# A graph attention kernel on one core: where the softmax's row sum is inverted, and which engine adds up the attention output

## The chip, the cores and the metric

The kernel runs on one core of one Trainium2 chip. The metric is the device time of the whole kernel in microseconds; the time before is the median of three runs. All events below are from one profiled execution, in microseconds from the start of its span.

Engines are called by the profile's names: PE (TensorE matmul), PEld (its weight loads), DVE (VectorE), ACT (ScalarE), POOL (GpSimd) and SP (SyncE, which issues DMAs here).

## The reference

There are N = 4096 nodes with D = 128 features, and a 4096x4096 adjacency matrix of int32 (ones and zeros). Two layers are added to x, each on relu(layernorm(x)):

```
h = relu(layernorm(x))                          # layer 1: masked dot-product attention
q, k, v = h @ Wq.T + bq, h @ Wk.T + bk, h @ Wv.T + bv
scores  = where(adj > 0, q @ k.T / sqrt(128), -9e15)
x = x + elu(softmax(scores) @ v)

h = relu(layernorm(x))                          # layer 2: additive attention
hw = h @ W; s1, s2 = hw @ a[:128], hw @ a[128:]
e = where(adj > 0, leaky_relu(s1[:, None] + s2[None, :], 0.01), -9e15)
x = x + hw + softmax(e) @ h
```

The change concerns the end of layer 1 alone: the division by the softmax's row sum, the bias bv (added behind the division, since a softmax row sums to one) and the elu.

## The kernel before

The kernel has four stages, told apart by the time at which they run in the profile.

1. 0 to about 60 us: x comes in, layernorm, and the products that give q, k and v. Each of q, k and v is kept as a high and a low part, so that products of reduced-precision operands keep float32's accuracy.
2. About 60 to 556 us: layer 1. The 4096 rows are T = 32 strips of 128. A strip is one **period** of every engine's program. Periods 0 to 3 and 28 to 31 are written out, and a loop runs over four periods at a time in between (`all_periods`). This is the stage that the change edits.
3. About 556 to 603 us: the second layernorm, the product with W and what depends on it.
4. About 603 to 841 us: layer 2's products (line 1248), strip by strip.

In stage 2 the order of every engine's work is written out by hand in `period(c, b, ahead)`, with s = 4c + b the strip; every engine executes its own list in order, and semaphores join the lists. For one strip:

- **SP** loads adj rows (2 MB of int32) two strips ahead, and stores mask bytes for layer 2.
- **POOL** turns adj into bytes (`make_bytes`, line 493) and bytes into a bf16 mask of 0 or -9e15 (`make_mask`, line 506). A pass takes a whole strip of 4096 columns. It also finishes the elu of the strip two back (`add_elu`, lines 512 to 515) and adds it to x.
- **PE** makes scores in four parts of 1024 columns (`make_scores`, lines 699 to 701, three products for each half), transposes the exponentials in eight blocks of 512 (`transpose(s, b, j)`, line 711), and multiplies each transposed block by v (`times_v(s, j)`, lines 721 and 722), which accumulates in `ps_acc`. Its order is: transpose 0, times_v 6 of the strip before, scores part 2 of s+1, transpose 1, times_v 7 of the strip before, scores part 3 of s+1, transpose 2, times_v 0, transpose 3, times_v 1, scores part 0 of s+2, transpose 4, times_v 2, transpose 5, times_v 3, transpose 6, times_v 4, scores part 1 of s+2, transpose 7, times_v 5.
- **DVE** adds the mask to each scores part and takes its maximum (`add_mask`, line 618, with a small gate at 616), takes the maximum over the parts (`find_max`, 624), and makes the low part of each transposed block (`low_part(s, j)`, line 630). PE's `times_v(s, j)` waits for `low_part(s, j)`. Between `low_part(s, 3)` and the mask addition for s+2 stands `normalise(s - 1)` (lines 633 to 643).
- **ACT** takes the exponentials (line 548, with the row sums), makes the high part of each block (`copy_pT`, 554), copies the accumulator of the strip before to SBUF behind block 1 (`acc_copy`, 560), and behind block 7 computes relu and exp for the elu (`elu_exp`, 565 to 568).

The accumulator has two halves of 128 columns, from the high and low parts of v. `normalise` takes the sum of four partial row sums (line 636), its reciprocal (637), adds the halves in SBUF (641), and multiplies by the reciprocal and adds the bias (642). The result `att` goes to ACT's `elu_exp`. A `Steps` helper puts a wait on DVE's own semaphore behind an instruction whose result the next one reads. `ps_acc` is one buffer: PE's `times_v(s, 0)` waits until ACT has copied strip s-1's accumulator.

Of the kernel before, what the change touches and what calls it, by code (L numbers as in the profile page):

```python
# [18 lines left out]
D = 128  # L19
# [217 lines left out]
def build(nc, x, adj, wq, bq, wk, bk, wv, bv, w1, a1, out):  # L237
# [7 lines left out]
    with ExitStack() as whole:  # L245
# [21 lines left out]
        row_sum = sb(whole, "row_sum", [D, 4, NP], F32)  # L267
        pool_gate = sb(whole, "pool_gate", [D, 5], F32)
        table_gate = sb(whole, "table_gate", [D, 3], F32)
        gate = sb(whole, "gate", [D, 4 * NP + 1], F32)  # L270
        inv_sum = sb(whole, "inv_sum", [D, 2], F32)

        const_ready, loaded, x_in = sem("const_ready"), sem("weights_loaded"), [sem(f"x_in{c}") for c in range(NC)]
# [10 lines left out]
        with ExitStack() as first:  # L284
# [7 lines left out]
            with ExitStack() as c1:  # L292
# [126 lines left out]
                sem("acc_out"), sem("att_ready"), sem("att_exp_ready"), sem("epilogue_done"))  # L419
            att_cut = sem("att_cut")  # L420
            own, pool_own = sem("vector_steps"), sem("pool_steps")
            gate_ready = sem("pool_gate_ready")
            bytes_ready, m_stored = sem("mask_bytes_ready"), [sem("even_masks_stored"), sem("odd_masks_stored")]
            STEPS = 3

            with ExitStack() as c2:
# [53 lines left out]
                def _(pool):  # L480
# [14 lines left out]
                    def make_mask(c, b):  # L495
# [10 lines left out]
                        nc.gpsimd.tensor_scalar(out, src, -NEG, NEG, ALU.mult, ALU.add).then_inc(mask_ready, 1)  # L506

                    def add_elu(s):

                        steps = Steps(pool, pool_own, 2 * s)  # L510
                        pool.wait_ge(att_exp_ready, s + 1)
                        steps.do(nc.gpsimd.tensor_tensor(att_exp[:], att_exp[:], ones[:], ALU.subtract))  # L512
                        steps.do(nc.gpsimd.tensor_tensor(att_exp[:], att_exp[:], att_pos[:], ALU.add))
                        xs = x_sb[:, s, :] if isinstance(s, int) else x_sb[:, bass.ds(s, 1), :].rearrange("p o f -> p (o f)")
                        nc.gpsimd.tensor_tensor(xs, xs, att_exp[:], ALU.add).then_inc(epi_done, 1)
# [7 lines left out]
                    def period(c, b, ahead):  # L523
                        last = isinstance(c, int) and c == NC - 1
                        if not (isinstance(c, int) and 4 * c + b < 2):
                            add_elu(4 * c + b - 2)
                        if not (last and b > 1):
                            make_mask(c + (b + 2) // 4, (b + 2) % 4)
                        if not (last and b > 0):
                            make_bytes(c + (b + 3) // 4, (b + 3) % 4)  # L530

                    all_periods(pool, period)
                    add_elu(T - 2)
                    add_elu(T - 1)

                @block.scalar
                def _(act):
# [17 lines left out]

                    def acc_copy(s):

                        act.wait_ge(pv_done, 8 * s + 8)
                        wait(act, att_ready, s)
                        nc.scalar.activation(acc_sb[:], ps_a[:], ACT.Copy).then_inc(acc_out, 1)  # L560

# [13 lines left out]
                    def period(c, b, ahead):  # L575
# [7 lines left out]
                        if not first:  # L583
                            acc_copy(s - 1)
                        copy_pT(s, 2)
# [15 lines left out]
                    all_periods(act, period)  # L601
                    acc_copy(T - 1)
                    elu_exp(T - 1)
# [3 lines left out]
                def _(dve):  # L607
# [24 lines left out]

                    def normalise(s, b):

                        steps = Steps(dve, own, STEPS * s)
                        steps.do(nc.vector.tensor_reduce(out=inv_sum[:, 0:1], in_=row_sum[:, b, :], axis=AX.X, op=ALU.add))
                        steps.do(nc.vector.reciprocal(inv_sum[:, 1:2], inv_sum[:, 0:1]))
                        dve.wait_ge(acc_out, s + 1)
                        wait(dve, att_exp_ready, s)
                        wait(dve, epi_done, s)  # L640
                        steps.do(nc.vector.tensor_tensor(acc_sb[:, 0, :], acc_sb[:, 0, :], acc_sb[:, 1, :], ALU.add))
                        nc.vector.scalar_tensor_tensor(out=att[:], in0=acc_sb[:, 0, :], scalar=inv_sum[:, 1:2], in1=bv_rep[:],
                                                       op0=ALU.mult, op1=ALU.add).then_inc(att_ready, 1)

# [13 lines left out]
                    def period(c, b, ahead):  # L658
                        s, bn = 4 * c + b, (b + 1) % 4
                        first = isinstance(c, int) and c == 0 and b == 0  # L660
                        low_part(s, 0)
                        if ahead:
# [6 lines left out]
                        low_part(s, 3)  # L669
                        if not first:  # L670
                            normalise(s - 1, (b + 3) % 4)
                        if ahead == 2:
# [6 lines left out]
                        low_part(s, 7)  # L679
                        if not first and not (isinstance(c, int) and s < 2):  # L680
                            moments_of(s - 2)

                    all_periods(dve, period)
                    normalise(T - 1, 3)
                    moments_of(T - 2)
                    dve.wait_ge(epi_done, T)
                    moments_of(T - 1)

# [615 lines left out]
```

## Time and profile before

| | us |
|---|---|
| median of 3 runs (lowest, highest) | 844.09 (843.63, 844.32) |
| the profiled execution's own time | 843.2 |
| its span, first to last instruction | 841.4 |
| PE busy | 771.5 |
| DVE busy | 618.2 |
| ACT busy | 566.9 |
| POOL busy | 303.6 |
| mean granted TensorE clock | 0.981 of full speed |

Matmuls are pipelined and their ends are modelled: the next one can start before the modelled end of the one in front, so the start-to-start distance tells what a matmul costs, and an idle time shown before a matmul begins at the modelled end. Idle times in square brackets are those of the engine, with what ended them.

### The profile page before, as it was taken

To read this page: it belongs to the slowest core of one execution; us is meant where nothing else is said; L and a number is where in the kernel's file an instruction comes from. 1 tells how busy PE (TensorE), PEld (TensorE's weight loads), DVE (VectorE), ACT (ScalarE), POOL (GpSimd) and SP (SyncE) were. 2 spreads that over 40 slices of the span, in tenths; PEclk is the share of its full clock that TensorE was granted. 3 is DMA by queue.
4 is the path that set the end of the run, shared out by engine and by line. 5 is a ranking of instruction groups with operands and counts; after the bars stand their busy time and mean duration, and the time that the engine had idled before them with its cause. 6 is when DMAs were issued, how large, how long until landed. Compare 5 with 4: busy or idle time off the path is not lost. (4 is left out here: it accounts for less than half of the span.)

```text
span 841.4 us, 17904 instructions
## 1 busy us (share of the span) xinstructions
PE 771.5 (92%) x6229; PEld 657.5 (78%) x6229; DVE 618.2 (73%) x1358; ACT 566.9 (67%) x1159; POOL 303.6 (36%) x238
## 2 busy tenths in 40 slices
PE   4979999999999999999999999968599999999997
PEld 2558888788788788788888888856488888888886
DVE  4847778778778778778778778659856755775672
ACT  5937767667667667667657657758588779777911
POOL 1087466466466466465465463124200000000000
PEclk9979999999999999999999999979799999999999
DMA  8069353643643543544544510045023344333200
GB/s 306 8 205 361 135 176 127 213 163 125 212 162 129 207 162 132 205 162 135 207 157 137 208 54 26 1 86 116 1 58 85 74 83 99 68 73 87 60 10 11
DMA packets 83338, 105.67 MB, mean 126 GB/s; under 512 B 68448, under 2 KB 75104, under 8 KB 79200
## 3 DMA queue, kind: packets, MB, share of 16 engines
q1 hardware_dynamic: 82560, 104.87, 39.8%
q8 instruction: 24, 0.39, 0.2%
q10 hardware_dynamic: 576, 0.26, 0.1%
q14 instruction: 18, 0.15, 0.1%
q0 software_dynamic: 160, 0.00, 0.0%
HBM read 69.47 MB, written 18.87 MB: 105 GB/s over the span
## 5 line engine op out<-in xcount | busy, mean ns | idle before, releaser
L554 ACT ACTIVATE pT_high<-ps_t 128x512 bf16<-128x512 f32 x256 | 151.8, 594 | 158.5 <-PE ps_t L711 157.6
L1248 PE MATMUL ps_x<-v,big 128*128 128x258 bf16 x2048 | 231.9, 274 | 2.3 <-issue 2.3
L1248 PEld LDWEIGHTS ps_x<-v,big 128*128 128x128 fp8e4 x2048 | 198.9, 98 | 32.5 <-issue 2.4
L721 PE MATMUL ps_acc<-v_parts,pT_high 128*128 128x256 bf16 x1024 | 196.7, 273 | 27.7 <-DVE pT_low L630 27.4
L618 DVE CUSTOM_DVE_ANT_0 scores<-ps_s,mask_neg 128x1024 f32<-128x1024 f32 x128 | 156.2, 1221 | 71.7 <-issue 71.7
L630 DVE TENSOR_TENSOR pT_low<-ps_t,pT_high 128x512 bf16<-128x512 f32 x256 | 171.3, 687 | 20.3 <-ACT pT_high L554 17.1
L722 PE MATMUL ps_acc<-v_parts,pT_low 128*128 128x128 bf16 x1024 | 182.7, 219 | 0.0
L548 ACT ACTIVATE scores<-scores,neg_max 128x1024 f32<-128x1024 f32 x128 | 146.2, 1144 | 13.6 <-DVE neg_max L624 13.6
L711 PE MATMUL ps_t<-ident,scores 128*128 128x128 f32 x1024 | 154.3, 273 | 0.5 <-DVE pT_low L630 0.5
L789 ACT ACTIVATE big<-s_block,s_col 128x512 fp8e4<-128x512 f32 x224 | 139.7, 718 | 0.0
L721 PEld LDWEIGHTS ps_acc<-v_parts,pT_high 128*128 128x128 bf16 x1024 | 100.1, 98 | 44.1 <-DVE pT_low L630 35.0
L711 PEld LDWEIGHTS ps_t<-ident,scores 128*128 128x128 f32 x1024 | 117.0, 140 | 18.7 <-DVE pT_low L630 0.5
L699 PE MATMUL ps_s<-k_hi,q_strip 128*128 128x512 f32 x256 | 113.0, 441 | 5.0 <-DVE row_max L618 2.8
L506 POOL TENSOR_SCALAR mask_neg<-mask_bytes 128x4096 bf16<-128x4096 uint8 x32 | 115.4, 3605 | 2.3
L493 POOL TENSOR_SCALAR mask_bytes<-adj_sb 128x4096 uint8<-128x4096 int32 x32 | 115.2, 3599 | 1.2 <-DMA mask_bytes_dram<-mask_bytes 0.6
L701 PE MATMUL ps_s<-k_hi,q_strip 128*128 128x512 f32 x256 | 102.3, 400 | 0.0
L722 PEld LDWEIGHTS ps_acc<-v_parts,pT_low 128*128 128x128 bf16 x1024 | 100.2, 98 | 2.5
L700 PE MATMUL ps_s<-k_lo,q_strip 128*128 128x512 f32 x256 | 101.3, 396 | 0.0
L512 POOL TENSOR_TENSOR att_exp<-att_exp,ones 128x128 f32<-128x128 f32 x32 | 14.6, 457 | 216.1 <-ACT att_exp L568 216.1
L1183 ACT ACTIVATE sums<-ps_x,ac 128x258 f32<-128x258 f32 x64 | 26.7, 469 | 63.8 <-PE ps_x L1248 63.8
L699 PEld LDWEIGHTS ps_s<-k_hi,q_strip 128*128 128x128 f32 x256 | 49.2, 192 | 12.9 <-DVE row_max L618 3.5
L701 PEld LDWEIGHTS ps_s<-k_hi,q_strip 128*128 128x128 f32 x256 | 49.0, 191 | 11.7
(133 smaller groups left out, 733.1 us busy)
## 6 DMA issues: line engine op xcount, KB each, us to landing
adj_sb<-in_adj SPq DMA_DIRECT2D x32, 2048.0 KB, 8.0
mask_bytes_dram<-mask_bytes SPq DMA_DIRECT2D x32, 512.0 KB, 8.7
x_sb<-in_x SPq DMA_DIRECT2D x8, 256.0 KB, 8.1
out<-res SPq DMA_DIRECT2D x32, 64.0 KB, 1.5
big<-mask_bytes_dram SPq DMA_TRANSPOSE x32, 4.5
raw_w<-in_L_gnn_Wq ACTq DMA_DIRECT2D x1, 64.0 KB, 3.1
raw_w<-in_L_gnn_Wk ACTq DMA_DIRECT2D x1, 64.0 KB, 3.6
raw_w<-in_L_gnn_Wv ACTq DMA_DIRECT2D x1, 64.0 KB, 4.9
```

The lines of the kernel that those rows point to most:

```text
L506: nc.gpsimd.tensor_scalar(out, src, -NEG, NEG, ALU.mult, ALU.add).then_inc(mask_ready, 1)
L548: nc.scalar.activation(sc, sc, ACT.Exp, bias=neg_max[:, bn:bn + 1], accum_out=row_sum[:, bn, k:k + 1]).then_inc(exp_done, 1)
L554: nc.scalar.activation(pT_high[j % 4][:], ps_t[j % 3][:], ACT.Copy).then_inc(pT_ready, 1)
L618: nc.vector.tensor_tensor_reduce(out=scores[bn % 2][:, part], in0=ps_s[k % 2][:], in1=mask[bn % 2][:, part], scale=1.0, scalar=LOWEST, op0 ...
L630: nc.vector.tensor_tensor(pT_low[j % 4][:], ps_t[j % 3][:], pT_high[j % 4][:], ALU.subtract).then_inc(low_ready, 1)
L699: nc.tensor.matmul(o, q[:, 0, :], k_hi[:, col], start=True, stop=False)
L701: last = nc.tensor.matmul(o, q[:, 1, :], k_hi[:, col], start=False, stop=True)
L711: last = nc.tensor.transpose(ps_t[j % 3][:, D * i:D * i + D], scores[b % 2][:, col:col + D], ident[:])
L721: nc.tensor.matmul(ps_a[:], pT_high[j % 4][:, part], v_parts[:, t, :, :], start=(t == 0), stop=False)
L722: last = nc.tensor.matmul(ps_a[:, 0, :], pT_low[j % 4][:, part], v_parts[:, t, 0, :], start=False, stop=(t == T - 1))
L789: return nc.scalar.activation(by_key_tile(lower[par], t), src.rearrange("p (s i) -> p s i", s=4), ACT.Sign, bias=s_col[:, t, 1:2], saturat ...
L1248: last = nc.tensor.matmul(ps_x[b % 2][k][:], by_key_tile(m, t)[:, b], v1[k][:, t, :].bitcast(BF16), start=(t == 0), stop=(t == T - 1))
```

## The change

`normalise` is taken apart. The sum of the row sums and its reciprocal (now `inverse_sum`) stand at the start of a period on DVE, and the reciprocal goes into a buffer with one column for odd and one for even strips. ACT's copy of the accumulator multiplies by it (`scale=`), so both halves arrive divided. POOL adds the halves and then the bias (`add_halves`), between its mask pass and its bytes pass. DVE's bn_stats for the second layernorm (`moments_of`) runs three strips behind instead of two, with a wait on the elu's end.

```diff
-        pool_gate = sb(whole, "pool_gate", [D, 5], F32)
+        pool_gate = sb(whole, "pool_gate", [D, 9], F32)
+        inv_by_parity = sb(whole, "inv_by_parity", [D, 2], F32)
...
-            STEPS = 3
+            STEPS = 1
...
+                    def add_halves(s, b):
+
+                        pool.wait_ge(acc_out, s + 1)
+                        if not isinstance(s, int):
+                            nc.gpsimd.tensor_tensor(pool_gate[:, 5 + b:6 + b], pool_gate[:, 0:1], pool_gate[:, 0:1], ALU.add)
+                        wait(pool, att_exp_ready, s)
+                        nc.gpsimd.tensor_tensor(acc_sb[:, 0, :], acc_sb[:, 0, :], acc_sb[:, 1, :], ALU.add).then_inc(halves_added, 1)
+                        pool.wait_ge(halves_added, s + 1)
+                        nc.gpsimd.tensor_tensor(att[:], acc_sb[:, 0, :], bv_rep[:], ALU.add).then_inc(att_ready, 1)
...
                             make_mask(c + (b + 2) // 4, (b + 2) % 4)
+                        if not (isinstance(c, int) and 4 * c + b < 1):
+                            add_halves(4 * c + b - 1, (b - 1) % 4)
                         if not (last and b > 0):
                             make_bytes(c + (b + 3) // 4, (b + 3) % 4)
 
                     all_periods(pool, period)
                     add_elu(T - 2)
+                    add_halves(T - 1, 3)
                     add_elu(T - 1)
...
-                    def acc_copy(s):
+                    def acc_copy(s, b):
 
                         act.wait_ge(pv_done, 8 * s + 8)
                         wait(act, att_ready, s)
-                        nc.scalar.activation(acc_sb[:], ps_a[:], ACT.Copy).then_inc(acc_out, 1)
+                        act.wait_ge(inv_ready, s + 1)
+                        nc.scalar.activation(acc_sb[:], ps_a[:], ACT.Copy, scale=inv_by_parity[:, b % 2:b % 2 + 1]).then_inc(acc_out, 1)
...
-                    def normalise(s, b):
+                    def inverse_sum(s, b):
 
                         steps = Steps(dve, own, STEPS * s)
                         steps.do(nc.vector.tensor_reduce(out=inv_sum[:, 0:1], in_=row_sum[:, b, :], axis=AX.X, op=ALU.add))
-                        steps.do(nc.vector.reciprocal(inv_sum[:, 1:2], inv_sum[:, 0:1]))
-                        dve.wait_ge(acc_out, s + 1)
-                        wait(dve, att_exp_ready, s)
-                        wait(dve, epi_done, s)
-                        steps.do(nc.vector.tensor_tensor(acc_sb[:, 0, :], acc_sb[:, 0, :], acc_sb[:, 1, :], ALU.add))
-                        nc.vector.scalar_tensor_tensor(out=att[:], in0=acc_sb[:, 0, :], scalar=inv_sum[:, 1:2], in1=bv_rep[:],
-                                                       op0=ALU.mult, op1=ALU.add).then_inc(att_ready, 1)
+                        wait(dve, acc_out, s - 1)
+                        nc.vector.reciprocal(inv_by_parity[:, b % 2:b % 2 + 1], inv_sum[:, 0:1]).then_inc(inv_ready, 1)
...
                         first = isinstance(c, int) and c == 0 and b == 0
+                        if not first:
+                            inverse_sum(s - 1, (b + 3) % 4)
                         low_part(s, 0)
...
                         low_part(s, 2)
                         low_part(s, 3)
-                        if not first:
-                            normalise(s - 1, (b + 3) % 4)
...
                         low_part(s, 7)
-                        if not first and not (isinstance(c, int) and s < 2):
-                            moments_of(s - 2)
+                        if not (isinstance(c, int) and s < 3):
+                            dve.wait_ge(epi_done, s - 2)
+                            moments_of(s - 3)
 
                     all_periods(dve, period)
-                    normalise(T - 1, 3)
-                    moments_of(T - 2)
-                    dve.wait_ge(epi_done, T)
-                    moments_of(T - 1)
+                    inverse_sum(T - 1, 3)
+                    for s in range(T - 3, T):
+                        dve.wait_ge(epi_done, s + 1)
+                        moments_of(s)
```

On DVE, in the middle of period 3 (the last one written out before the loop), before the change: the two `low_part` for blocks 2 and 3, `normalise`, the mask addition for part 0 of strip 5 (lines 616 and 618), and the `low_part` for blocks 4 to 6.

```order
L630 TENSOR_TENSOR pT_low<-ps_t,pT_high 128x512 [waits pT_ready] x2
L636 TENSOR_REDUCE inv_sum<-row_sum 128x1
L637 RECIPROCAL inv_sum<-inv_sum 128x1 [waits vector_steps]
L641 TENSOR_TENSOR acc_sb<-acc_sb 128x128 [waits att_exp_ready,epilogue_done,acc_out,vector_steps]
L642 SCALAR_TENSOR_TENSOR att<-acc_sb,inv_sum,bv_rep 128x128 [waits vector_steps]
L616 MEMSET gate 128x1 [waits scores_ready,p_transposed,mask_ready]
L618 ISA scores,row_max<-ps_s,mask_neg 128x1024
L618 ISA row_max 128x1
L630 TENSOR_TENSOR pT_low<-ps_t,pT_high 128x512 [waits pT_ready] x3
```

The same place with the change; `low_part` is now at line 645 and the mask addition at 631 and 633.

```order
L645 TENSOR_TENSOR pT_low<-ps_t,pT_high 128x512 [waits pT_ready] x2
L631 MEMSET gate 128x1 [waits scores_ready,p_transposed,mask_ready]
L633 ISA scores,row_max<-ps_s,mask_neg 128x1024
L633 ISA row_max 128x1
L645 TENSOR_TENSOR pT_low<-ps_t,pT_high 128x512 [waits pT_ready] x3
```

All four instructions have left this place. Two of them stand at the start of the period, between `low_part(s - 1, 7)` and `low_part(s, 0)`:

```order
L645 TENSOR_TENSOR pT_low<-ps_t,pT_high 128x512 [waits pT_ready]
L651 TENSOR_REDUCE inv_sum<-row_sum 128x1
L653 RECIPROCAL inv_by_parity<-inv_sum 128x1 [waits acc_out,vector_steps]
L645 TENSOR_TENSOR pT_low<-ps_t,pT_high 128x512 [waits pT_ready]
L631 MEMSET gate 128x1 [waits scores_ready,p_transposed]
L633 ISA scores,row_max<-ps_s,mask_neg 128x1024
```

DVE no longer waits for `acc_out` of the strip just copied, only for that of the strip before it.

On POOL, one period before the change: three steps of the elu, the mask pass and the bytes pass.

```order
L512 TENSOR_TENSOR att_exp<-att_exp,ones 128x128 [waits att_exp_ready]
L513 TENSOR_TENSOR att_exp<-att_exp,att_pos 128x128 [waits pool_steps]
L515 TENSOR_TENSOR x_sb<-x_sb,att_exp 128x128 [waits pool_steps]
L506 TENSOR_SCALAR mask_neg<-mask_bytes 128x4096 [waits scores_masked,mask_bytes_ready]
L493 TENSOR_SCALAR mask_bytes<-adj_sb 128x4096 [waits odd_masks_stored,adj_in_odd]
```

And with it:

```order
L523 TENSOR_TENSOR att_exp<-att_exp,ones 128x128 [waits att_exp_ready]
L524 TENSOR_TENSOR att_exp<-att_exp,att_pos 128x128 [waits pool_steps]
L526 TENSOR_TENSOR x_sb<-x_sb,att_exp 128x128 [waits pool_steps]
L507 TENSOR_SCALAR mask_neg<-mask_bytes 128x4096 [waits scores_masked,mask_bytes_ready]
L515 TENSOR_TENSOR acc_sb<-acc_sb 128x128 [waits att_exp_ready,acc_out]
L517 TENSOR_TENSOR att<-acc_sb,bv_rep 128x128 [waits acc_halves_added]
L494 TENSOR_SCALAR mask_bytes<-adj_sb 128x4096 [waits odd_masks_stored,adj_in_odd]
```

Two additions have come in, the first of which waits for ACT's copy; in the loop a gate of one column (`pool_gate`) stands before them. The bytes pass is queued behind them. ACT's and PE's lists keep their order.

## Rows read from the trace of the kernel before

**Rows 1.** Windows: busy us of each engine, granted clock, DMA share, GB/s.
```profile
61.00:552.00 491.00, 462.83 (x3802) 403.53 (x3802) 389.71 (x814) 330.34 (x694) 264.14 (x199) 1.00 0.45 155
612.00:841.00 229.00, 223.42 (x2018) 194.58 (x2015) 143.31 (x310) 160.00 (x290) 0.00 (x0) 1.00 0.30 65
```

**Rows 2.** Waits of PE, stage 2's largest: us in total, times, longest.
```profile
PE ps_acc L721 <- DVE pT_low L630: 27.4, 30, 1.0
```

**Rows 3.** Timeline of PE: start us, us, what; first, a middle, last stall.
```profile
102.08 0.28 PE L721 MATMUL ps_acc<-v_parts,pT_high 128*128 128x256 bf16 x1 [0.55 <-DVE pT_low L630]
...
304.49 0.61 PE L711 MATMUL ps_t<-ident,scores 128*128 128x128 f32 x4
306.10 0.28 PE L721 MATMUL ps_acc<-v_parts,pT_high 128*128 128x256 bf16 x1 [1.00 <-DVE pT_low L630]
...
510.17 0.28 PE L721 MATMUL ps_acc<-v_parts,pT_high 128*128 128x256 bf16 x1 [0.55 <-DVE pT_low L630]
```

**Rows 4.** Timeline of DVE ahead of the stall at 306.10.
```profile
300.23 1.49 DVE L630 TENSOR_TENSOR pT_low<-ps_t,pT_high 128x512 bf16<-128x512 f32 x2
301.64 0.15 DVE L636 TENSOR_REDUCE inv_sum<-row_sum 128x1 f32<-128x4 f32 x1
...
302.08 1.75 DVE L641 TENSOR_TENSOR acc_sb<-acc_sb 128x128 f32<-128x128 f32 x1
...
304.20 1.23 DVE L618 CUSTOM_DVE_ANT_0 scores<-ps_s,mask_neg 128x1024 f32<-128x1024 f32 x1
...
305.36 1.88 DVE L630 TENSOR_TENSOR pT_low<-ps_t,pT_high 128x512 bf16<-128x512 f32 x3
```

**Rows 5.** Timeline of POOL, bytes pass, elu and mask pass.
```profile
300.09 3.60 POOL L493 TENSOR_SCALAR mask_bytes<-adj_sb 128x4096 uint8<-128x4096 int32 x1
310.12 0.46 POOL L512 TENSOR_TENSOR att_exp<-att_exp,ones 128x128 f32<-128x128 f32 x1 [6.43 <-ACT att_exp L568]
...
311.99 3.61 POOL L506 TENSOR_SCALAR mask_neg<-mask_bytes 128x4096 bf16<-128x4096 uint8 x1
```

**Rows 6.** Timeline of DVE, line 641 in periods 1, 2, 29 and 30.
```profile
83.91 0.29 DVE L641 TENSOR_TENSOR acc_sb<-acc_sb 128x128 f32<-128x128 f32 x1
...
98.45 1.43 DVE L641 TENSOR_TENSOR acc_sb<-acc_sb 128x128 f32<-128x128 f32 x1
...
521.83 0.29 DVE L641 TENSOR_TENSOR acc_sb<-acc_sb 128x128 f32<-128x128 f32 x1
...
536.38 0.29 DVE L641 TENSOR_TENSOR acc_sb<-acc_sb 128x128 f32<-128x128 f32 x1
```

**Rows 7.** Timeline: copy of block 4, accumulator copy, PE's times_v 0.
```profile
303.17 0.58 ACT L554 ACTIVATE pT_high<-ps_t 128x512 bf16<-128x512 f32 x1
...
313.15 0.39 ACT L560 ACTIVATE acc_sb<-ps_acc 128x256 f32<-128x256 f32 x1
...
314.82 0.27 PE L721 MATMUL ps_acc<-v_parts,pT_high 128*128 128x256 bf16 x1
```

**Rows 8.** Timeline of DVE where a period starts.
```profile
310.82 0.69 DVE L630 TENSOR_TENSOR pT_low<-ps_t,pT_high 128x512 bf16<-128x512 f32 x1 [0.38 <-ACT pT_high L554]
312.06 1.22 DVE L618 CUSTOM_DVE_ANT_0 scores<-ps_s,mask_neg 128x1024 f32<-128x1024 f32 x1 [0.55 <-issue]
```

**Rows 9.** Single lines: duration ns min/median/max, first and last start.
```profile
L630 DVE TENSOR_TENSOR pT_low<-ps_t,pT_high x256: 678/686/694, 64.8 to 550.8; 128x512 bf16<-128x512 f32 x128
L1183 ACT ACTIVATE sums<-ps_x,ac x64: 454/470/481, 613.1 to 835.8; 128x258 f32<-128x258 f32 x64
```

**Rows 10.** Timeline of the end of stage 2: POOL, DVE, ACT.
```profile
552.01 0.45 POOL L513 TENSOR_TENSOR att_exp<-att_exp,att_pos 128x128 f32<-128x128 f32 x1
552.54 0.45 POOL L515 TENSOR_TENSOR x_sb<-x_sb,att_exp 128x128 f32<-128x128 f32 x1
553.13 0.29 DVE L641 TENSOR_TENSOR acc_sb<-acc_sb 128x128 f32<-128x128 f32 x1 [1.15 <-POOL x_sb L515]
...
553.84 0.31 ACT L565 ACTIVATE att_neg<-att 128x128 f32<-128x128 f32 x1 [1.00 <-DVE att L642]
```

More of the change, by code:

```diff
@@ L419, in build @@
                 sem("acc_out"), sem("att_ready"), sem("att_exp_ready"), sem("epilogue_done"))
-            att_cut = sem("att_cut")
-            own, pool_own = sem("vector_steps"), sem("pool_steps")
+            att_cut, halves_added = sem("att_cut"), sem("acc_halves_added")
+            own, pool_own, inv_ready = sem("vector_steps"), sem("pool_steps"), sem("inv_sum_ready")
             gate_ready = sem("pool_gate_ready")
             bytes_ready, m_stored = sem("mask_bytes_ready"), [sem("even_masks_stored"), sem("odd_masks_stored")]
-            STEPS = 3
+            STEPS = 1
             with ExitStack() as c2:
@@ L583, in period @@
                         if not first:
-                            acc_copy(s - 1)
+                            acc_copy(s - 1, b + 1)
                         copy_pT(s, 2)
@@ L601, in _ @@
                     all_periods(act, period)
-                    acc_copy(T - 1)
+                    acc_copy(T - 1, 3)
                     elu_exp(T - 1)
```

## The prediction, made blind

> **What bounds the kernel now.** I read the windows by stage first. Stage 2, from 61 to 552 us, is 491 us long; PE is busy for 463 of them at a granted clock of 1.00, DVE for 390, ACT for 330, POOL for 264 [rows 1]. So PE bounds the stage, and what can be had without less matmul work is about 28 us of pauses. The waits of PE come next: 27.4 us, 30 times, before the first matmul of a `times_v`, on DVE's `low_part` [rows 2]. The timeline of PE says which: once in a period, behind transpose 6, `times_v(s, 4)` begins 1.61 us after it instead of following it at once (304.49 to 306.10, shown as 1.00 us of idle), for want of `low_part(s, 4)` [rows 3].
>
> The timeline of DVE says why that is late [rows 4]. `low_part` 2 and 3 end at 301.72. Then stand the sum and reciprocal (301.64 to 302.08), the addition of the halves at line 641, 1.75 us, line 642, and the mask addition from 304.20; only at 305.36 do `low_part` 4 to 6 run. Block 4 had been copied by ACT at 303.17 + 0.58 = 303.75 [rows 7]. So `low_part(s, 4)` is 1.6 us late.
>
> Line 641 doesn't need 1.75 us. In period 1 it took 0.29 us, in period 29 and 30 too [rows 6]. In the period shown POOL's bytes pass runs from 300.09 to 303.69 [rows 5], and line 641 ends at 302.08 + 1.75 = 303.83, just behind it. The instruction is held until the pass is over. Nothing else on DVE is: the 256 `low_part`, whose one SBUF input is the high part, take 678 to 694 ns throughout, POOL busy or not [rows 9].
>
> The Trainium skill (SBUF — State Buffer, Who interferes with whom) has this as a rule: a DVE instruction with two SBUF inputs and a GpSimd instruction that reads SBUF exclude each other for the whole instruction. The rule would also hold line 642 and spare all that stays on DVE in the loop, where each instruction has at most one SBUF input; the durations agree.
>
> **The size of the stall, from periods without it.** Line 641 starts at 83.91 and 98.45, a period of 14.54 us; at 521.83 and 536.38, 14.55 us [rows 6]. Both have no stall of PE in between. From 98.45 to 521.83 lie 27 periods in 423.38 us, 15.68 each. Each holds one stall, the first at 102.08, the last at 510.17; three show 0.55 us, 24 show 1.00 to 1.03 [rows 3]. Without stalls these 27 periods would take 27 x 14.55 = 392.9 us. The difference is 423.4 - 392.9 = 30.5 us. The sum of the shown idle is a little less, since the modelled end of the transpose hides some 0.17 us of each. The 14.55 us are also a floor: PE has no pause left in such a period, and the change takes nothing off PE.
>
> **The change part by part.**
>
> *Removed from the middle of the period on DVE:* the sum and reciprocal (0.44 us), the held addition (1.75 + 0.04), and line 642 (303.87 to 304.20, 0.33): the whole distance from 301.64 to 304.20, 2.56 us [rows 4]. What is late next? The mask addition for s+2 needs PE's scores part, which ends at about 302.5: it would run from 302.5 to 303.7. Block 4's copy is ready at 303.75, so `low_part(s, 4)` runs 303.75 to 304.44. PE would ask for it 0.44 us after transpose 6 begins, at 304.93. It is there half a microsecond early, and the stall goes completely: -30.5 us. The real periods without a stall say the same, and they had even 0.29 us of line 641 and line 642 in the way.
>
> *Added at the start of the period on DVE:* sum and reciprocal, 0.44 us by the distance 301.64 to 302.08, and a wait on the copy of the strip before the last, nearly a period old. Queued behind it is `low_part(s, 0)`, which now waits 0.38 us for ACT and has another 0.55 us of idle behind it before the mask addition, which waits for PE's scores [rows 8]. PE needs `low_part(s, 0)` only at `times_v(s, 0)`, 314.82 [rows 7], over 3 us later. Cost 0. If the cover were gone, 0.44 us a period, 31 x 0.44 = 14 us, is the upper bound.
>
> *ACT's copy with a scale:* 0.39 us without [rows 7]. With a scale from a column, ACT's copies of the same kind in layer 2 take 0.47 us for 258 columns [rows 9], so +0.08. It would end at 313.62; PE's `times_v(s, 0)` wants it at 314.82 [rows 7]. Hidden, with 1.2 us to spare. The new wait on the reciprocal is met 2 us before, and the one on `att_ready` now asks for POOL's addition of the period before: due about 11 us earlier. Cost 0 in the loop.
>
> The Trainium skill (ScalarE: Activation LUTs, What ACT_TABLE_LOAD costs) has a scale or bias read from a column at about 93 ns more than an immediate; by that the copy would take an estimated 0.48 us, which changes nothing in the sum.
>
> *POOL's two additions:* the elu's additions of the same shape take 0.46 us and follow each other at 0.53 to 0.54 us [rows 5, 10]. With a gate of a column (0.26 us) the two take 1.3 us, behind the mask pass, which ends at 315.60 [rows 5]. ACT's copy is there at 313.6, so POOL needn't wait. `att` is ready at about 316.9; ACT's elu wants it seven microseconds later, at the period's end. POOL's work in a period becomes about 1.9 (elu and gate) + 3.7 + 1.3 + 3.9 = 10.8 us, of 14.55. The mask pass stands ahead of the additions and isn't moved; the bytes pass ends 1.3 us later and is read by POOL itself 3.7 us after that, and by the DMAs, which have two periods. Cost 0.
>
> On this edit the Trainium skill speaks against the change: its GPSIMD Engine Reference, 4.1 Engine selection, keeps element-wise additions on VectorE, with GpSimd about two times slower for two inputs. The rows have 0.29 us on DVE undisturbed and 0.46 on POOL; by the rule it would be an estimated 0.58 each, off the critical path as well, but for the tail.
>
> *The moments* go from two strips behind to three: same count, and the wait is on an elu that ended a period before. 0. In the first periods POOL's bytes pass for strip 4 must wait for ACT's copy, some 5 us later than now, with over 8 us until POOL needs it: 0.
>
> *The tail* is on the path: behind the last `times_v` everything waits for everything. Now: POOL's elu for strip 30 ends at 552.99, DVE adds at 553.13, ACT starts at 553.84 [rows 10]. Then: POOL starts its first addition at 553.07, the second 0.53 us later, ends 0.45 us after that at 554.05, ACT at about 554.1. +0.3 us; the bounds are 0 and, with both additions at their unhidden 0.54 + 0.54 and one more handover, +0.5.
>
> **Sum.** -30.5 + 0.3 = -30.2 us. The profiled execution took 843.2 (span 841.4), which gives 813.0 (811.2). The median of the runs shown is 0.9 above it: forecast 813.9 us. Its own range, with bounds of 1.5 us below (the run's own 0.9 and a little idle of DVE and ACT set free in the last, irregular periods) and 3 us above (up to 0.1 us a period of new waits), is 812.4 to 817.
>
> **Rivals.**
>
> *Half of the stall comes back.* The half microsecond that `low_part(s, 4)` has in hand is eaten up, because something else is held on DVE or ACT reaches block 4 later. For it: the margin is small against 1.2 us of stall. Against: periods 1 and 29 had 0.64 us more on DVE at this very place and no stall [rows 6]. If 0.5 us stay in each of 27 periods: 813.9 + 13.5 = 827 us.
>
> *The change doesn't move the stall,* because line 641 was only the place where a late ACT or PE was waited for, and `low_part(s, 4)` takes over the wait. Then it is 844 us, within the 0.2% (1.7 us) that a measurement of this kernel can't tell from none. Against: block 4's copy was ready at 303.75, 1.6 us before it was used [rows 4, 7].
>
> *Slower: a ring through POOL.* ACT's copy waits for POOL's addition of the period before, POOL's addition for ACT's copy, POOL's two passes stand in the same queue, and DVE's mask addition waits for a pass. The place is the gap between POOL's 10.8 us and the period; it decides when POOL's round exceeds 15.7 us, the period of now. For it: POOL's round grows, and its additions read two SBUF tensors while DVE is busy four fifths of the time; if each were held as line 641 was, 1.3 us more each, POOL is at 13.4 us, and a hold of all its five additions, 6.5 us, brings 17.3 us with the mask late. 29 rounds of 17.3 instead of 15.7: 844 + 46 = 890 us at the worst; at 16.2 us a round, 858. Against: POOL's passes take 3.60 and 3.61 us beside a working DVE [rows 5], and its elu additions 0.45 to 0.46 in the loop and at the idle end alike [rows 5, 10].
>
> A fall of the granted clock, now that PE never pauses, would cost too; stage 4 has PE busy 223 of 229 us at 1.00 [rows 1], which speaks against it. I count it with the second rival.
>
> **How the numbers follow.** Forecast 0.87; half of it back 0.07; no change 0.02; slower 0.04. Faster by over 0.2%: 0.87 + 0.07 = 0.94; same 0.02; slower 0.04. For 8 in 10 the range needs the forecast's own with a little more on the side where all the unknowns lie: 812 to 819.
>
> **What would show it.** In the changed profile the wait of PE's `ps_acc` on `pT_low` should be 1 to 3 us in total instead of 27.4, mostly outside the loop; periods should be 14.55 us; no DVE instruction of the loop should vary in length; POOL's additions should take 0.46 us, and POOL should still idle over 3 us before each elu. The accumulator copy should take 0.47 us. The forecast is wrong if `low_part` 4 still ends after 0.44 us behind transpose 6, if PE shows a new wait for ACT's copy, or if PE's clock drops in stage 2.

## The result, and the profile after

| | before | after |
|---|---|---|
| median us (lowest, highest), runs | 844.21 (843.63, 844.52), 4 | 814.33 (811.28, 815.24), 4 |
| ratio (95% interval) | 1 | 0.9641 (0.9615 to 0.9666) |
| profiled execution: own time, span | 843.2, 841.4 | 811.28, 809.5 |

The change makes the kernel 3.6% faster: 29.9 us between the medians. The windows of the changed kernel are cut at its own stage ends. As in [rows 1], a line has the window, its length, the busy us (and instructions) of PE, PEld, DVE, ACT and POOL, the granted clock, the DMA share and GB/s.

```profile
61.00:522.00 461.00, 457.35 (x3798) 404.04 (x3796) 336.49 (x750) 331.87 (x693) 295.15 (x289) 1.00 0.47 164
582.00:809.50 227.50, 221.66 (x2002) 193.06 (x1999) 141.99 (x309) 158.68 (x288) 0.00 (x0) 1.00 0.30 65
```

Stage 2 has PE busy for 457 of 461 us, at the same granted clock. The waits of PE on the accumulator's matmuls, which answer to [rows 2] (us in total, times, longest):

```profile
PE ps_acc L732 <- DVE pT_low L645: 1.6, 3, 0.8
PE ps_acc L732 <- ACT acc_sb L575: 0.2, 1, 0.2
```

27.4 us have become 1.6: three waits of 0.3, 0.5 and 0.85 us in the written-out periods at either end, which the kernel before had too. None is left in the inner periods. The middle of one period on DVE, which answers to [rows 4]; `low_part` is now line 645, the mask addition 633:

```profile
299.16 1.49 DVE L645 TENSOR_TENSOR pT_low<-ps_t,pT_high 128x512 bf16<-128x512 f32 x2
301.44 1.22 DVE L633 CUSTOM_DVE_ANT_0 scores<-ps_s,mask_neg 128x1024 f32<-128x1024 f32 x1 [0.78 <-issue]
301.46 0.06 DVE L631 MEMSET gate<- 128x1 f32 x1
302.58 0.08 DVE L633 DVE_READ_ACCUMULATOR2_ANT row_max<- 128x1 f32 x1
302.70 0.69 DVE L645 TENSOR_TENSOR pT_low<-ps_t,pT_high 128x512 bf16<-128x512 f32 x1
```

DVE has 0.78 us of idle where 2.56 us of work and holding stood (the profile names no releaser for it; PE's last product of this scores part ends at 301.39, just ahead of the mask addition), and `low_part(s, 4)` ends at 303.39. On PE, transpose 6 of the same period and the `times_v(s, 4)` that used to stall, which answer to [rows 3]:

```profile
303.43 0.61 PE L722 MATMUL ps_t<-ident,scores 128*128 128x128 f32 x4
303.87 0.27 PE L732 MATMUL ps_acc<-v_parts,pT_high 128*128 128x256 bf16 x1
```

0.44 us lie between them, not 1.61, and no idle time is shown: `low_part(s, 4)` is 0.48 us ahead of its use. The period's start on DVE, in two successive periods (one row of each for the distance, then what stands behind it), answers to [rows 8]:

```profile
293.57 0.14 DVE L651 TENSOR_REDUCE inv_sum<-row_sum 128x1 f32<-128x4 f32 x1
...
308.12 0.14 DVE L651 TENSOR_REDUCE inv_sum<-row_sum 128x1 f32<-128x4 f32 x1
308.30 0.16 DVE L653 RECIPROCAL inv_by_parity<-inv_sum 128x1 f32<-128x1 f32 x1
308.41 0.69 DVE L645 TENSOR_TENSOR pT_low<-ps_t,pT_high 128x512 bf16<-128x512 f32 x1
309.81 1.22 DVE L633 CUSTOM_DVE_ANT_0 scores<-ps_s,mask_neg 128x1024 f32<-128x1024 f32 x1 [0.70 <-issue]
```

308.12 - 293.57 = 14.55 us, the period. DVE is still idle for 0.70 us, until PE's last product of the scores part ends at 309.77. POOL in the same period, which answers to [rows 5]:

```profile
293.32 0.46 POOL L523 TENSOR_TENSOR att_exp<-att_exp,ones 128x128 f32<-128x128 f32 x1 [4.15 <-ACT att_exp L583]
...
295.19 3.61 POOL L507 TENSOR_SCALAR mask_neg<-mask_bytes 128x4096 bf16<-128x4096 uint8 x1
298.88 0.20 POOL L513 TENSOR_TENSOR pool_gate<-pool_gate 128x1 f32<-128x1 f32 x1
299.02 0.46 POOL L515 TENSOR_TENSOR acc_sb<-acc_sb 128x128 f32<-128x128 f32 x1
299.56 0.46 POOL L517 TENSOR_TENSOR att<-acc_sb,bv_rep 128x128 f32<-128x128 f32 x1
299.98 0.19 POOL L493 TENSOR_TENSOR pool_gate<-pool_gate 128x1 f32<-128x1 f32 x1
300.13 3.60 POOL L494 TENSOR_SCALAR mask_bytes<-adj_sb 128x4096 uint8<-128x4096 int32 x1
```

POOL's round is 10.4 us; in the loop it idles 4.15 us before each elu.

Where the 31.9 us between the two spans lie, by the first `times_v` (before 65.54, after 64.29), the first step of the second layernorm (556.78, 525.35), the first matmul of line 1248, 1259 in the changed kernel (603.48, 572.09), and the end (841.4, 809.5): 1.25 us in stage 1, which the change doesn't touch and where executions of one kernel differ by as much; 491.24 - 461.06 = 30.18 us in stage 2; 46.70 against 46.74 us in stage 3; 0.5 us in stage 4.

### The profile page after: what moved, and what is told of

It reads as the page before. It is cut to its first block and busy times, and to the rows that moved or that the text cites. A ratio compares the mean times of both kernels' runs of the same rounds, so it can differ in the third digit from the quotient of the medians.

```text
span 809.5 us, 17843 instructions
## 1 busy us (share of the span) xinstructions
PE 765.8 (95%) x6229; PEld 658.3 (81%) x6229; DVE 565.6 (70%) x1294; ACT 568.7 (70%) x1159; POOL 335.4 (41%) x326
## 5 line engine op out<-in xcount | busy, mean ns | idle before, releaser
L645 DVE TENSOR_TENSOR pT_low<-ps_t,pT_high 128x512 bf16<-128x512 f32 x256 | 176.3, 690 | 46.7 <-ACT pT_high L568 43.0
```

Source lines behind the costliest of these rows:

```text
L645: nc.vector.tensor_tensor(pT_low[j % 4][:], ps_t[j % 3][:], pT_high[j % 4][:], ALU.subtract).then_inc(low_ready, 1)
```

## The experiments

There were twelve runs, in three sets; each is compared with the kernel before in its own set. A period is a start-to-start distance in the loop. The **block** is what stands on DVE between `low_part(s, 3)` and the mask addition for s+2, from its first instruction's start to the mask addition's, or to its own end where DVE idles behind it.

**The changed kernel again (after_again).** 

> The changed kernel itself, timed again beside the others. All theories: about 814 us, in a span of some 4 us between its runs. It serves as the comparison for the three kernels that run with it.

Measured 815.05 us (814.61 to 815.95, 5 runs) against 843.57: ratio 0.9662 (0.9648 to 0.9676). A third time (after_third), beside the last experiments: 

> The changed kernel, timed once more beside the version with one reduction on DVE. All theories: 814 to 815.5 us.

 It took 813.46 us (811.71 to 816.06, 5 runs), 0.5 below the expected range, ratio 0.9651 (0.9635 to 0.9666).

**One reduction on DVE for halves and bias (e3_three).** An edit of the changed kernel: the bias stands as a third block beside the two halves, which ACT's copy has scaled. (Dots stand for lines that are not shown; the comments say what a line is for.)

```diff
-                acc_sb = sb(c2, "acc_sb", [D, 2, D], F32)
+                acc_sb = sb(c2, "acc_sb", [D, 3, D], F32)      # [:, 2, :] holds the bias
...
+                        nc.vector.tensor_reduce(out=att[:], in_=acc_sb[:].rearrange("p k f -> p f k"), axis=AX.X,
+                                                op=ALU.add).then_inc(att_ready, 1)    # DVE, behind low_part(s, 3)
...
-                            add_halves(4 * c + b - 1, (b - 1) % 4)                    # POOL
```

> The changed kernel, with the halves and the bias added on DVE again, in the old place behind low_part 3, but by one reduction over three blocks of a single SBUF tensor (the two halves and a copy of the bias). Theory (what hurt was that line 641, with two SBUF inputs, was held until POOL's pass ended): the reduction is never held, takes 0.35 to 0.5 us every time, and falls into the 0.78 us in which DVE waits for the scores at this place; PE has no stall, 813.5 to 814.5 us, even 0.3 to 0.5 us below the changed kernel, since the last strip is added without POOL. Rival (any work of DVE between low_part 3 and the mask addition delays low_part 4): 0.4 us a period, 826 us. Rival (POOL's pass holds every DVE instruction that reads the accumulator's copy): 844 us.

Measured 812.92 us, ratio 0.9636 (0.9621 to 0.965), 0.6 below the expected range. The reduction, over 32 calls (duration ns min/median/max, first and last start):

```profile
L647 DVE TENSOR_REDUCE att<-acc_sb x32: 584/589/601, 83.3 to 522.4; 128x128 f32<-128x384 f32 x32
```

It is never held, at the very place where line 641 was held for 1.46 us, and beside POOL's bytes pass as before: in one period it runs from 301.61 to 302.19, the pass from 300.07 to 303.67. (It takes 0.59 us; I had expected 0.35 to 0.5.) PE has no stall in the inner periods: 14.55 us each. So neither a place nor DVE's reading of the accumulator's copy was the matter.

**POOL's bytes pass in eight pieces, all else as before (e1_pieces).**

```diff
-                        nc.gpsimd.tensor_scalar(mask_bytes[b % 2][:], adj_sb[b % 2][:], 1.0, 0.0, ALU.min, ALU.max).then_inc(bytes_ready, 1)
+                        for i in range(8):
+                            piece = slice(512 * i, 512 * i + 512)
+                            last = nc.gpsimd.tensor_scalar(mask_bytes[b % 2][:, piece], adj_sb[b % 2][:, piece], 1.0, 0.0, ALU.min, ALU.max)
+                        last.then_inc(bytes_ready, 1)
```

> The kernel before, with POOL's bytes pass cut into eight passes of 512 columns; DVE keeps all of its work in the old place. Theory: line 641 is held for one piece at the most, so it takes 0.3 to 0.8 us instead of 1.75, PE's stall is gone or below 0.2 us a period, and the time is 814 to 819 us without any of the change. Rival (DVE's work in this place is simply too long, 2.56 us): 835 to 844 us, since only the hold is shorter. Rival (the pieces cost POOL so much that its round becomes the bound): POOL's round of 9.5 us grows by 7 times 0.1 us, no effect.

Measured 817.42 us, ratio 0.9691 (0.9675 to 0.9707). DVE's block in one period and POOL's pieces beside it, and DVE's two instructions over all:

```profile
304.96 0.15 DVE L639 TENSOR_REDUCE inv_sum<-row_sum 128x1 f32<-128x4 f32 x1
...
305.41 0.50 DVE L644 TENSOR_TENSOR acc_sb<-acc_sb 128x128 f32<-128x128 f32 x1
305.94 0.58 DVE L645 SCALAR_TENSOR_TENSOR att<-acc_sb,inv_sum,bv_rep 128x128 f32<-128x128 f32 x1
306.45 1.21 DVE L621 CUSTOM_DVE_ANT_0 scores<-ps_s,mask_neg 128x1024 f32<-128x1024 f32 x1
```
```profile
303.43 4.72 POOL L495 TENSOR_SCALAR mask_bytes<-adj_sb 128x512 uint8<-128x512 int32 x8
```
```profile
L644 DVE TENSOR_TENSOR acc_sb<-acc_sb x32: 291/498/749, 85.5 to 527.1; 128x128 f32<-128x128 f32 x32
L645 DVE SCALAR_TENSOR_TENSOR att<-acc_sb,inv_sum,bv_rep x32: 352/580/585, 85.9 to 527.4; 128x128 f32<-128x128 f32 x32
```

Eight pieces in 4.72 us are 0.59 us each, so one ends at about 305.79 and the next at 306.38; the two instructions end at 305.91 and 306.52. Each of the two instructions with two SBUF inputs is now held for 0.2 us, to the end of a piece, instead of one of them to the end of the pass. The block is 304.96 to 306.45, 1.49 us, the period 14.64. The hold is the cause of most of the stall: 26.2 of the 28.5 us that the change brings in the same set of runs come back with DVE's program untouched. (The pieces cost POOL 1.1 us a period, 4.72 against 3.60, where 0.7 was expected; POOL has the room.)

**The addition as a reduction, line 642 kept (e2_reduce).**

```diff
-                        steps.do(nc.vector.tensor_tensor(acc_sb[:, 0, :], acc_sb[:, 0, :], acc_sb[:, 1, :], ALU.add))
+                        steps.do(nc.vector.tensor_reduce(out=acc_sum[:], in_=acc_sb[:].rearrange("p k f -> p f k"), axis=AX.X, op=ALU.add))
```

> The kernel before, with the addition of the halves as a reduction over one SBUF tensor; line 642 behind it keeps its two SBUF inputs. Theory (two SBUF inputs against a POOL instruction that reads SBUF): the reduction takes 0.3 to 0.4 us, and line 642 is held in its place until POOL's pass ends, some 1.3 us instead of 0.35; 843 to 845 us, as before. Rival (it is the tensor_tensor instruction, or the reading of what ACT has just written, that is slow): line 642 keeps 0.35 us and the time falls to 814 to 816 us.

Measured 831.49 us, ratio 0.9859 (0.9841 to 0.9878): neither number. DVE in one period, and POOL's pass beside it:

```profile
311.04 0.15 DVE L637 TENSOR_REDUCE inv_sum<-row_sum 128x1 f32<-128x4 f32 x1
...
311.48 0.43 DVE L642 TENSOR_REDUCE acc_sum<-acc_sb 128x128 f32<-128x256 f32 x1
311.95 1.30 DVE L643 SCALAR_TENSOR_TENSOR att<-acc_sum,inv_sum,bv_rep 128x128 f32<-128x128 f32 x1
313.18 1.21 DVE L619 CUSTOM_DVE_ANT_0 scores<-ps_s,mask_neg 128x1024 f32<-128x1024 f32 x1
```
```profile
309.50 3.60 POOL L494 TENSOR_SCALAR mask_bytes<-adj_sb 128x4096 uint8<-128x4096 int32 x1
```

The durations are those of the theory: the reduction is free, and the hold has gone over to the next instruction with two SBUF inputs, 0.35 to 1.30 us, which ends 0.15 us behind the pass (313.10). The time is not, because I had taken the block's end as fixed. With line 641 held, 0.35 us of line 642 still followed the pass; now nothing does. The block is 2.14 us, the period 15.28, so 0.45 us less in each of 27 periods, 12 us. So the instruction's kind isn't the cause, which the rival said, nor is it the reading of what ACT has just written, since line 643 reads what DVE wrote; the two SBUF inputs are.

The Trainium skill (SBUF — State Buffer, Who interferes with whom) says this of a DVE instruction with two SBUF inputs beside a GpSimd instruction that reads SBUF, and spares those with at most one, outside the modes in which DVE uses both its ports; these two experiments agree, and they show it for `scalar_tensor_tensor` as well. In all these rows POOL's pass had begun first; no run shows the other order.

**Sum and reciprocal at the period's start, nothing else (e6_early).** Lines 636 and 637 move as in the change; 641 and 642 stay.

```diff
+                        if not first:
+                            inverse_sum(s - 1, (b + 3) % 4)      # the sum and the reciprocal
                         low_part(s, 0)
```

> The kernel before, with the sum and the reciprocal (0.44 us) moved to the start of the period, as the change does; lines 641 and 642 stay on DVE in the old place. Theory: line 641 starts 0.44 us earlier, and is held until the same end of POOL's pass, so it takes 2.2 us instead of 1.75 and the block still ends at the same moment: 843 to 845 us, no gain. Rival (the length of the work on DVE is what counts): 0.44 us less in each of 27 periods, 832 us.

Measured 843.88 us, ratio 0.9999 (0.999 to 1.0009): no gain.

```profile
302.23 2.20 DVE L645 TENSOR_TENSOR acc_sb<-acc_sb 128x128 f32<-128x128 f32 x1
304.47 0.35 DVE L646 SCALAR_TENSOR_TENSOR att<-acc_sb,inv_sum,bv_rep 128x128 f32<-128x128 f32 x1
304.77 0.06 DVE L616 MEMSET gate<- 128x1 f32 x1
304.80 1.22 DVE L618 CUSTOM_DVE_ANT_0 scores<-ps_s,mask_neg 128x1024 f32<-128x1024 f32 x1
```
```profile
300.69 3.60 POOL L493 TENSOR_SCALAR mask_bytes<-adj_sb 128x4096 uint8<-128x4096 int32 x1
```

The addition is at hand 0.44 us earlier and is held 0.44 us longer, to the end of the pass at 304.29. The block is 2.57 us, as it was. Here work ahead of the held instruction was free; this is the counterpart of e2_reduce, where work behind it was not.

**Filler on DVE in the changed kernel (e4_fill5, e4_fill13).** Small reductions with one SBUF input, in every period, in the old place; `n` is 5 or 13.

```diff
                         low_part(s, 3)
+                        if not first:
+                            for i in range(n):
+                                nc.vector.tensor_reduce(out=filler[:, 16 * b + i:16 * b + i + 1], in_=ident[:], axis=AX.X, op=ALU.add)
```

> The changed kernel with five small reductions (128x128, one SBUF input, result unused) on DVE in the old place between low_part 3 and the mask addition, in every period; they can't be held by POOL. Theory: DVE's block in this place is hidden up to some 1.4 us, whatever it is made of (a block of 2.56 us cost 1.18 us a period, one of 2.14 us 0.75, one of 1.49 us 0.09); five reductions take 1.0 to 1.3 us, so no stall, 814 to 816 us. Rival (POOL's pass and DVE's work disturb each other in another way than by the hold, and the hold was the whole cause): also 814 to 816.

> The same with thirteen small reductions, about 2.6 us a period. Theory (the length of the block counts, beyond 1.4 us one for one): PE waits for low_part 4 again, 1.2 us a period, 31 periods, 848 to 856 us, although nothing is held. Rival (only the hold by POOL's pass matters): 814 to 818 us.

Measured 815.37 us, ratio 0.9655 (0.963 to 0.968), with five; 847.13 us, ratio 1.0044 (1.003 to 1.0057), with thirteen, 0.9 below the expected range. The thirteen on DVE, and then two successive stalls of PE:

```profile
302.59 2.59 DVE L685 TENSOR_REDUCE filler<-ident 128x1 f32<-128x128 f32 x13
305.11 1.22 DVE L634 CUSTOM_DVE_ANT_0 scores<-ps_s,mask_neg 128x1024 f32<-128x1024 f32 x1
```
```profile
307.00 0.28 PE L736 MATMUL ps_acc<-v_parts,pT_high 128*128 128x256 bf16 x1 [0.94 <-DVE pT_low L646]
322.66 0.28 PE L736 MATMUL ps_acc<-v_parts,pT_high 128*128 128x256 bf16 x1 [0.94 <-DVE pT_low L646]
```

Nothing is held here (the reductions take 0.20 us from start to start), and the old stall is back at the old place, with a period of 15.67 us. So it is the length of the block that PE waits for; the hold only made it long. The kernel is even 0.4% slower than the one before, with a block 0.04 us shorter, because the filler makes the block as long in the written-out periods: 29 periods take 15.67 us, where the kernel before had 24 full stalls and three of 0.55 us. All blocks so far:

| kernel | block us | period us | over 14.55 |
|---|---|---|---|
| changed kernel | 0 | 14.55 | 0 |
| e3_three | 0.6 | 14.55 | 0 |
| e4_fill5 | 0.97 | 14.55 | 0 |
| e1_pieces | 1.49 | 14.64 | 0.09 |
| e2_reduce | 2.14 | 15.28 | 0.73 |
| e4_fill13 | 2.52 | 15.67 | 1.12 |
| before | 2.56 | 15.73 | 1.18 |
| e6_early | 2.57 | 15.74 | 1.19 |

Block less 1.40 us is the stall, within 0.02 us, for blocks with and without a hold, where the block is longer than that; the 1.40 was read from the first set of runs, before the fillers ran. The changed profile has 1.26 of the 1.40 us in two places: DVE's idle time before the mask addition (0.78) and the lead of `low_part(s, 4)` (0.48). Another 0.10 is the way from the mask addition's start to that `low_part`, 1.26 us (301.44 to 302.70) behind idle time and 1.16 us (304.20 to 305.36) without [rows 4]. The last 0.04 us is not accounted for.

**Filler at the period's start (e7_start).** Four of the same reductions behind `inverse_sum`.

> The changed kernel with four more small reductions on DVE at the start of a period, behind the sum and reciprocal, 0.8 us. Theory (the start of a period has over 0.7 us of idle DVE, and nothing of PE's waits on it soon): 814 to 816 us. Rival of the prediction (work at the period's start isn't hidden): 0.8 us a period, 31 periods, 839 us.

Measured 813.27 us, ratio 0.9633 (0.9617 to 0.9648), 0.7 below the expected range.

```profile
308.92 0.85 DVE L675 TENSOR_REDUCE filler<-ident 128x1 f32<-128x128 f32 x4
309.68 0.69 DVE L646 TENSOR_TENSOR pT_low<-ps_t,pT_high 128x512 bf16<-128x512 f32 x1
310.35 1.22 DVE L634 CUSTOM_DVE_ANT_0 scores<-ps_s,mask_neg 128x1024 f32<-128x1024 f32 x1
```

The idle time before the mask addition is used up, and nothing is late (stage 2 takes 461.07 us, the changed kernel's time): at least 0.8 us more than the change's 0.44 are hidden there.

**A longer round on POOL (e5_pool36, e5_pool54).** Behind `add_halves`, unused passes over k_lo: one of 4096 columns, or one of 4096 and one of 2048.

```diff
                             add_halves(4 * c + b - 1, (b - 1) % 4)
+                            for a, w in [(0, 4096), (4096, 2048)]:    # e5_pool36: only the first
+                                nc.gpsimd.tensor_scalar(filler[:, a:a + w], k_lo[:, 0:w].bitcast(I32), 1.0, 0.0, ALU.min, ALU.max)
```

> The changed kernel with one more pass of 4096 columns (3.6 us, result unused) on POOL behind its two additions. POOL now idles 4.15 us before each elu. Theory (POOL's round has 4.15 us to spare): 0.5 us is left, no stall, 814 to 816 us. Rival of the prediction (a ring through POOL's queue sets the period early): 820 us and more.

> The same with a pass of 4096 and one of 2048 columns, about 5.4 us. Theory (the ring decides once POOL's round is longer than PE's 14.55 us): the round is 10.4 + 5.5 = 15.9 us and becomes the period, 28 periods of the inner part, 814 + 28 x 1.35 = 845 to 855 us, with PE waiting for DVE and DVE for the mask. Rival (masks are made far enough ahead for the ring not to bite): 814 to 818 us.

Measured 813.95 us, ratio 0.9647 (0.9628 to 0.9666), with one; 842.23 us, ratio 0.9986 (0.9973 to 0.9999), with both. With one pass POOL still idles:

```profile
309.02 0.46 POOL L524 TENSOR_TENSOR att_exp<-att_exp,ones 128x128 f32<-128x128 f32 x1 [0.57 <-ACT att_exp L586]
```

With both it doesn't; two rounds of POOL, then what DVE waits for:

```profile
298.89 3.60 POOL L508 TENSOR_SCALAR mask_neg<-mask_bytes 128x4096 bf16<-128x4096 uint8 x1
...
314.66 3.60 POOL L508 TENSOR_SCALAR mask_neg<-mask_bytes 128x4096 bf16<-128x4096 uint8 x1
```
```profile
302.65 0.06 DVE L634 MEMSET gate<- 128x1 f32 x1 [2.50 <-POOL mask_neg L508]
```

The danger that the prediction's third rival named exists, though no ring of waits is needed for it: POOL is simply never out of work, its round of 15.77 us sets the period, and the mask is late. It came out 3 us below the expected range because the masks start with a lead: PE's first such stall is at 162.61, so it bites in 24 periods and not in 28. The change left it 4.15 us away.

**The reduction again, beside the changed kernel (e3_again).** 

> The kernel with one reduction on DVE for halves and bias, timed again beside the changed kernel. Theory: stage 2 is 0.4 to 0.5 us shorter than the changed kernel's, from the end of the last strip, so the median is 0.3 to 1 us below it; the 2.1 us between the medians of the first comparison are for the most part scatter between executions.

Measured 812.59 us (810.99 to 812.97), ratio 0.9622 (0.9608 to 0.9636), and the changed kernel beside it 813.46: 0.9 us less, after 2.1 us less the first time. Stage 2, from the first `times_v` to the second layernorm, is 65.33 to 525.95 and 67.05 to 527.67, 460.62 us both times; the changed kernel's is 461.06 to 461.07 three times. The end of stage 2 with the reduction, in the first of its two profiles (e3_three):

```profile
522.39 0.59 DVE L647 TENSOR_REDUCE att<-acc_sb 128x128 f32<-128x384 f32 x1 [0.98 <-ACT acc_sb L563]
522.90 0.48 DVE L657 BATCH_NORM_STATS2 bn<-x_sb 128x6 f32<-128x128 f32 x2
525.35 0.29 DVE L657 BATCH_NORM_STATS2 bn<-x_sb 128x6 f32<-128x128 f32 x1 [1.97 <-POOL x_sb L517]
```

From the last copy of the accumulator (521.88) to the last bn_stats are 3.47 us, and 3.46 in the second profile; the changed kernel takes 3.91. That gives the 0.44 us and is shown; that the rest between the medians is scatter is likely and not shown. This version has the lower median in both comparisons, but the intervals of its ratio and the changed kernel's overlap a little in both, so its lead rests on the 0.44 us in the profiles.

## Why the prediction was right

- **What bounds stage 2.** Right: PE, with one stall a period, and 14.55 us a period as the floor. From the first to the thirtieth of ACT's copies of the accumulator in the changed kernel, every distance is 14.55 or 14.56 us.
- **The cause of the stall.** Right, and now shown and not only read: the hold goes when the second SBUF input goes (e3_three), it moves to the next instruction with two of them (e2_reduce), and it shrinks with POOL's instruction (e1_pieces). The prediction showed POOL's pass only beside a held line 641; beside the ones of 0.29 us at 83.91, 521.83 and 536.38 POOL runs nothing in the trace of before (idle from 78.7 to 90.8, from 519.4 to 528.8, and from 530.3 to 543 us), which bears it out. One refinement: the prediction took out the whole block of 2.56 us and didn't ask how much of it mattered. e6_early shows that 0.44 us of the block counted for nothing by themselves, e2_reduce that what stands behind the held instruction counts in full, and e4_fill13 that 2.5 us of plain work in the place would have cost as much as the hold.
- **-30.5 us for the stall.** Stage 2 is 30.18 us shorter in all, tail included; -30.2 was forecast. That it fits to 0.02 us is luck: the tail cost 0.1 us less than forecast, and a wait for ACT's copy of 0.2 us (below) was not in the sum.
- **Sum and reciprocal at the start, 0.** Right, with more to spare than the 0.55 us named (e7_start).
- **ACT's scaled copy, +0.08 us, hidden.** It takes 474 ns, against 386 before: 0.09. In the loop it is hidden. In the last written-out period it isn't quite: PE waits 0.21 us for it once (the second of the waits above), which I had not counted and which the prediction named as a sign of being wrong; it never comes in the loop. The Trainium skill (ScalarE: Activation LUTs, What ACT_TABLE_LOAD costs) has about 93 ns for such an operand; the trace has 88.
- **POOL's additions, 0.46 us each, no effect.** Right: 453 to 465 ns, against 291 for line 641 on DVE when it isn't held, and 4.15 us of idle left where "over 3" was forecast. POOL's round is 10.4 us, not 10.8.
- **The tail, +0.3 us.** From the last accumulator copy's start to the last bn_stats: 552.45 to 556.18 before, 3.73 us; 520.84 to 524.75 after, 3.91. So +0.2.
- **The rivals.** None came true. The first one's worry, a lead of half a microsecond, was a true number (0.48), but the room for new work in that place is 1.40 us, for DVE's 0.78 us of idle lie in front of it. The periods 1 and 29 that spoke against this rival had more in the way than the prediction counted: with the sum and the reciprocal their block was 1.03 us, still below 1.40.
- **The median.** 813.9 forecast, 814.33 measured; the profiled execution was 1.7 us faster than 813.0, by 1.25 us of stage 1 and 0.5 of stage 4, for which the forecast had no term. The three medians of the changed kernel are 814.33, 815.05 and 813.46, so that the first lies within 0.4 us of the forecast is in part luck.

## What to carry to other kernels

When one engine's instruction is much longer at one place than at another, look at what its neighbour is doing at the moment it ends: here a 0.29 us addition ended with a 3.6 us pass of GpSimd in nearly every period, and the few periods in which no pass ran beside it gave the gain to the microsecond. Moving the work to the other engine is one cure; giving the instruction a single SBUF input (a reduction over stacked blocks) or cutting the neighbour's pass into pieces are others; the pieces take four lines of code and left 0.09 us of stall a period. And the time freed by such a cure is the stall, not the hold: here 1.40 us of the 2.56 us block were hidden, work ahead of the held instruction cost nothing, and work behind it cost in full as long as the block was beyond those 1.40 us.

## What the runs showed that was not expected

Runs of one kernel differ by up to 4.6 us. The changed kernel took 811.28 to 815.24 us in the first four runs, 814.61 to 815.95 in the next five and 811.71 to 816.06 in the last five; the kernel before took 843.63 to 844.52 in the first set and 842.58 to 845.66 over 15 runs of the last. Two profiled executions of the changed kernel with spans of 809.5 and 812.8 us (the first and after_again) differ by 1.2 us in stage 1, by 1.5 us in stage 3 (46.74 against 48.28 us) and by 0.6 us in stage 4, not in stage 2. In stage 3 the difference is the granted clock of one stretch of 15 us that begins 5 us behind the second layernorm's start; first the faster, then the slower execution:

```profile
530.00:545.00 15.00, 14.36 (x82) 11.19 (x81) 11.34 (x25) 11.55 (x35) 6.20 (x6) 0.83 1.07 213
```
```profile
531.30:546.30 15.00, 15.00 (x71) 12.30 (x70) 9.12 (x24) 9.18 (x28) 4.68 (x5) 0.63 1.06 209
```

PE had waited 7.5 us for the layernorm just before, and 0.83 and 0.63 are means over two levels: in both executions the clock fell from 2.4 to 1.2 GHz during that wait. In the faster one it was back at 2.4 GHz 6.7 us after PE had resumed (from 528.31 to 535.01), in the slower one 13.0 us after (529.57 to 542.54), with PE at work all the time.

The 14 traces of this case, of all the kernels here, are of these two kinds. In eight of them the clock fell 2.4 to 3.8 us before PE resumed, and was back 6.4 to 7.8 us after. In the six others it fell 3.9 to 4.6 us before, and was back 12.5 to 13.2 us after; their stage 3 is about 1.5 us longer. The earlier fall goes with the later return every time. PE's wait is 7.1 to 7.5 us in all of them, so its length doesn't tell the two kinds apart, and what sets the moment of the fall stays open.
